# Fused mixer layers on one core: residual sum on TensorE and ScalarE, a shorter routing choice, first group's step sizes ahead of the others

## Chip, core, metric

One core of a Trainium2 chip runs the whole program in one launch. The metric is the device time in microseconds, the median of the runs of one kernel on one chip. TensorE is called PE below, VectorE DVE, ScalarE ACT, GpSimd POOL; SP is the engine that issues most DMAs.

## What is computed

Two layers over 8 sequences of 512 tokens and 256 channels. The change touches only the first half of the first layer, which ends with the routing of the first mixture of experts. Cut to that half:

```python
c   = layernorm((gelu(x @ Wsoma) * sigmoid(temporal(x) @ Wtemp)) @ Wout)   # conditioner
xc, z = split(c @ W_in)                      # 512 + 512 channels
xc  = silu(conv4(xc)); dt, B, C = split(xc @ W_x, [64, 80])
delta = softplus(dt @ W_dt + b_dt)           # per token and channel
for n in 16 states:                          # h, y: 512 channels x 512 tokens
    h_n[t] = exp(delta[t] * A_n) * h_n[t-1] + delta[t] * xc[t] * B_n[t]
    y[t]  += C_n[t] * h_n[t]
x = x + ((y + D * xc) * silu(z)) @ W_out     # residual sum
y0 = x @ Wsub[subject] + bsub
logits = y0 @ Wg + bg; probs = softmax(logits / 5); top 2 of 8; gates normalised
```

`temporal(x)` is a blend of eight causal moving averages of `x * sigmoid(gate)`. Ties at the second largest probability go to the lower expert number.

## The kernel before

The program is a row of blocks, each with one instruction stream for each engine. Streams meet only through semaphores, and every stream is issued in the order in which it is written. The block that matters here is the one that `mixers` makes, with a prologue for batch 0, the eight batches, and after it the short block of `route_last`.

**The scan.** A batch has four groups of 128 channels, and a group four steps. A step `N` (16 in a batch, 128 in all) handles one group and four of the states: DVE makes the input `delta*x*B` (`into`, a product of 128 x 2048), runs the recurrence as one scan over 2048 elements (`scan`), and multiplies the result of the step before by C (`out`). The order in a step is scan N, out N-1, into N+1, and then the small work of `tasks(b, n)`. ACT makes the decays `dA` of step N+2 (`decays`, four exponentials of 511 elements), in `dA`'s two buffers, so decays of N+2 wait for the end of scan N. PE sums the products of the states (`add_state`).

**Around the scan.** While batch b is scanned, its neighbours are worked on in slots `n` = 0 to 15: `k` = b-1 is finished (out product with `Wo`, residual sum `add_out`, subject product, routing), `kc` = b+1 is prepared (conditioner, convolution, delta), and `ke` = b+2 has its gate made. Each engine has a function `tasks(b, n)` that writes out what it does in slot n. `behind` gives k (none for b = 0), `next_up` gives kc (none for b = 7) and ke (none from b = 6).

**The conditioner's averages.** PE turns the gated input (`turn_gated`, line 813), ACT scales and copies it (`scale_turned`, line 920), PE averages (line 822) and takes the block ends (line 829), for eight averages and two halves each, through slots 15, 0, and 2 to 6. These alternate strictly: PE, ACT, PE, ACT. Then come `copy_ends`, `tempo_ready` (line 930), the product with `Wtemp` and the sigmoid `temporal_gate` (line 935). DVE multiplies with it in `soma_gated` (line 988). The products of batch k stand in the same two streams: out product, subject product (`xm,ws`) in two halves, and the logits (`w_Wg,W0u`, 16 small matmuls), on which DVE's `route_maxima` (line 1052) waits.

**Delta to the scan.** `delta_parts` makes |v| and relu(v) on ACT, then exp and ln; `delta_ready` (lines 1002, 1004) sums and multiplies on DVE. The scan needs each channel on four partitions' rows, so delta and u go to HBM (`store_first_group` for group 0, `store_groups` for the other three) and come back spread (`spread_delta`, line 1105, and `spread_u`, line 1114, four DMAs each).

Of the kernel before, what the change touches and what calls it, by code (L numbers as in the profile page):

```python
# [95 lines left out]
def build(nc, a, out):  # L96
    with ExitStack() as ctx:
# [90 lines left out]
        def load_first(st):  # L188
            def sb(name, shape, dt=F32):
# [25 lines left out]
            S4 = sb("S4", [P, LINE])  # L215
            modT = sb("modT", [P, TT, NTR])
# [14 lines left out]
                    mix, Dg, Dc, Rm, S4, modT, f)  # L231
# [190 lines left out]
        def choose_rest(dve, ch, gate_exp, probs, tmp, srt, small, E, K, k=0):  # L422
# [18 lines left out]
            for t in range(TT):  # L441
                ch.step(dve.tensor_tensor_scan(tmp[:, 2, t, :], tmp[:, 1, t, :], tmp[:, 1, t, :], 0.0,
                                               ALU.add, ALU.max))
# [117 lines left out]
        def place_pairs(dve, ch, M, v, bank, limit=False, k=0):  # L561
# [18 lines left out]
            ch.link(dve.tensor_tensor(tmp[:, 1], tmp[:, 1], tmp[:, 0], ALU.mult))  # L580
# [204 lines left out]
        def gate_product(pe, c, k, j):  # L785
            if j == 0:
                pe.wait_ge(c_hg, k + 1)
                pe.wait_ge(c_ctx, DC * (k + 1))
            elif k:
                pe.wait_ge(m_pre, JI * k)  # L790
# [89 lines left out]
        def z_product(pe, k):  # L880
            pe.wait_ge(m_pre, JI * (k + 1))
# [80 lines left out]
        def delta_parts(act, c, k):  # L962
            for j in range(JI):
                act.wait_ge(m_dl, JI * k + j + 1)
                act.activation(c.ab[:, j, :], ps[:, 4 + j, :], ACT.Abs, bias=bdt[:, j:j + 1]).then_inc(m_abs, 1)
                act.activation(c.pre[:, j, :], ps[:, 4 + j, :], ACT.Relu, bias=bdt[:, j:j + 1]).then_inc(m_pre, 1)
# [3 lines left out]
            act.activation(c.ab[:, :, :], c.ab[:, :, :], ACT.Ln, bias=1.0).then_inc(m_ln, 1)  # L970
# [22 lines left out]

        def delta_ready(dve, m, c, k):
            dve.wait_ge(m_pre, JI * (k + 1))
            dve.wait_ge(m_ln, k + 1)
            if k == 0:
                dve.tensor_tensor(c.dl[:, 0, :], c.pre[:, 0, :], c.ab[:, 0, :], ALU.add).then_inc(m_dlr, 1)
                dve.wait_ge(m_dlr, 1)
                dve.tensor_tensor(c.u[:, 0, :], c.dl[:, 0, :], m.xs[:, 0, :], ALU.mult).then_inc(m_u, 1)  # L1000
            j = 1 if k == 0 else 0
            dve.tensor_tensor(c.dl[:, j:, :], c.pre[:, j:, :], c.ab[:, j:, :], ALU.add).then_inc(m_dlr, 1)
            dve.wait_ge(m_dlr, k + 2)
            dve.tensor_tensor(c.u[:, j:, :], c.dl[:, j:, :], m.xs[:, j:, :], ALU.mult).then_inc(m_u, 1)
# [52 lines left out]
        def route_choice(dve, v, ch, k):  # L1057
            choose_rest(dve, ch, r_ex, v.pb[:, :, :], v.tmp, v.srt, v.small, E0, K0, k)
            finish_choice(dve, ch, v.tmp, v.small, E0, K0)
            ch.link(dve.tensor_copy(v.chosen[:, :, :], v.tmp[:, 0]))  # L1060
# [1659 lines left out]
```

## Time and profile before

| | |
|---|---|
| median of 3 runs | 3658.3 us (3652.96 to 3664.64) |
| the profiled execution, its own time | 3662.31 us |
| its span, first to last instruction | 3660.6 us |
| busy in the span | PE 3198.4, DVE 2149.7, ACT 1577.8, POOL 637.8 us |
| mixer block's scans | 144.2 to 1431.4 us |
| TensorE's clock, mean over the span | 0.933 of full |

The spans of the engines overlap, so busy times don't add up. The mixer block takes the first 1446 us, and there DVE is busy in nine tenths or more of nearly every fortieth of the span. What follows (experts, attention, the second layer) isn't touched by the change.

### The profile page before, as it was taken

Reading aid. Unit: us, or ns where it says so; the run is one execution under the profiler, and the core shown is the slowest. Engines: PE = TensorE matmul, PEld = TensorE weight load, DVE = VectorE, ACT = ScalarE, POOL = GpSimd, SP = SyncE. Lnnn points to the kernel's source line nnn. Section 1 sums busy time; section 2 is a strip of 40 time slices with the busy share of each in tenths; the row PEclk is TensorE's granted clock in tenths of the full one; section 3 lists DMA queues with packets and bytes.
Section 4 is the critical chain, followed back from the end, with each engine's and each line's share of the span. In section 5 each row is a group of like instructions: output and inputs, shape, how many; then the busy total and the mean of one; then the engine's idle time right before and its main releaser. Section 6 shows DMA issues by size and latency. Waiting matters only on the chain. (4 is left out here: it accounts for less than half of the span.)

```text
span 3660.6 us, 40917 instructions
## 1 busy us (share of the span) xinstructions
PE 3198.4 (87%) x12812; PEld 1754.9 (48%) x12813; DVE 2149.7 (59%) x2703; ACT 1577.8 (43%) x3071; POOL 637.8 (17%) x767
## 2 busy tenths in 40 slices
PE   8788888888888743899799999999999999978996
PEld 5445353534445211566444444444444444436875
DVE  2499999999999998222233444443434343432334
ACT  4565666666665531333232424242424242423443
POOL 0000202012020202333100202020202020215772
PEclk9898998989898865899899999999999999988998
DMA  2446555555646555322300101010101010055547
GB/s 63 116 120 165 144 146 150 141 153 139 161 122 161 147 140 190 99 67 65 137 0 22 36 22 36 21 37 21 37 21 36 22 37 3 31 208 164 157 156 271
DMA packets 193227, 362.86 MB, mean 99 GB/s; under 512 B 28274, under 2 KB 85106, under 8 KB 191922
## 3 DMA queue, kind: packets, MB, share of 16 engines
q1 hardware_dynamic: 164514, 296.19, 28.2%
q0 software_dynamic: 20352, 57.17, 4.2%
q10 hardware_dynamic: 8208, 7.54, 0.6%
q8 instruction: 85, 1.39, 0.2%
q14 instruction: 68, 0.56, 0.1%
HBM read 250.53 MB, written 110.28 MB: 99 GB/s over the span
## 5 line engine op out<-in xcount | busy, mean ns | idle before, releaser
L1665 DVE TENSOR_TENSOR_SCAN hs<-dA,hs 128x2048 f32<-128x2048 f32 x128 | 566.2, 4423 | 7.1
L452 POOL COPY rows<-slot 128x64 f32<-128x64 f32 x48 | 16.6, 376 | 2592.3 <-DVE new_pl L589 2553.4
L2255 PE MATMUL ps<-pT,V 128*128 128x512 f32 x1024 | 450.7, 593 | 0.9 <-DVE pT L2423 0.9
L1506 ACT ACTIVATE dA<-dl,w_An 128x511 f32<-128x511 f32 x512 | 326.6, 711 | 144.3 <-DVE hs L1665 132.9
L1353 PE MATMUL ps<-hs,w_S 128*32 128x512 f32 x1024 | 176.0, 723 | 169.3 <-DVE hs L1671 169.3
L1657 DVE TENSOR_TENSOR hs<-u,bb 128x2048 f32<-128x2048 f32 x128 | 292.5, 2285 | 19.5 <-DMA u<-ud 9.9
L2255 PEld LDWEIGHTS ps<-pT,V 128*128 128x128 f32 x1024 | 189.6, 190 | 221.1 <-issue 214.8
L1671 DVE TENSOR_TENSOR hs<-hs,cb 128x2048 f32<-128x2048 f32 x128 | 290.4, 2269 | 0.0
L1825 POOL DMA_INDIRECT slots<-og,idt x232 | 241.8, 1042 | 260.2 <-DVE og L1913 197.2
L448 POOL DMA_INDIRECT sorted<-rows,new_pl x192 | 268.2, 1397 | 63.6 <-issue 44.8
L2330 ACT ACTIVATE pp<-ps,nm 128x512 f32<-128x512 f32 x256 | 172.3, 685 | 215.1 <-DVE nm L2406 215.1
L409 PE MATMUL ps<-w_Wv,y 128*128 128x512 f32 x512 | 230.8, 597 | 0.0
L2405 DVE TENSOR_REDUCE mx<-ps 128x4 f32<-128x2048 f32 x64 | 146.4, 2288 | 132.4 <-PE ps L2231 132.4
L813 PE MATMUL ps<-w_mix,W0u 128*128 128x128 f32 x1024 | 165.0, 311 | 52.6 <-ACT W0u L920 39.6
L813 PEld LDWEIGHTS ps<-w_mix,W0u 128*128 128x128 f32 x1024 | 144.4, 216 | 103.1 <-ACT W0u L920 70.0
L920 ACT ACTIVATE W0u<-ps,w_modT 128x256 f32<-128x256 f32 x256 | 106.7, 468 | 176.0 <-PE ps L813 160.6
L409 PE MATMUL ps<-W1u,xT 128*128 x640 | 167.3, 384 | 0.0
L2358 ACT ACTIVATE pT<-ps 128x512 f32<-128x512 f32 x128 | 77.3, 604 | 197.4 <-PE ps L2243 197.4
L2243 PEld LDWEIGHTS ps<-ident,pp 128*128 128x128 f32 x1024 | 115.1, 141 | 90.5 <-issue 61.6
L2423 DVE COPY pT<-ps 128x512 f32<-128x512 f32 x128 | 88.4, 691 | 114.3 <-PE ps L2243 113.7
L822 PE MATMUL ps<-W0u 128*128 128x128 f32 x1024 | 144.5, 291 | 8.8 <-ACT sz L1514 8.8
L1353 PEld LDWEIGHTS ps<-hs,w_S 128*32 128x32 f32 x1024 | 27.8, 117 | 254.3 <-DVE hs L1671 209.6
(355 smaller groups left out, 5389.0 us busy)
## 6 DMA issues: line engine op xcount, KB each, us to landing
bb<-bcd SPq DMA_DIRECT2D x128, 256.0 KB
cb<-bcd SPq DMA_DIRECT2D x128, 256.0 KB
dl<-dld SPq DMA_DIRECT2D x128, 256.0 KB, 6.6
u<-ud SPq DMA_DIRECT2D x128, 256.0 KB, 8.3
xg<-sorted SPq DMA_DIRECT2D x232, 136.0 KB, 2.1
slots<-zeros SPq DMA_DIRECT2D x136, 128.0 KB, 3.8
qrg<-slots SPq DMA_DIRECT2D x32, 512.0 KB, 16.4
rg<-slots SPq DMA_DIRECT2D x32, 256.0 KB, 4.8
```

What stands on the lines that cost most here:

```text
L409: last = pe.matmul(dst, lhsT, rhs, start=(i == 0), stop=(i == len(pairs) - 1))
L448: pool.indirect_dma_start(M.sorted, bass.IndirectOffsetOnAxis(new_pl[:, t, i:i + 1], 0), v.rows[:, i % v.R, t, :], None).then_inc(M.listed ...
L813: ins = pe.matmul(ps[:, turn_bank(k, h), q % 2 * D + j * P:q % 2 * D + (j + 1) * P], c.gated[:, j, q * P:(q + 1) * P], mix[:, j, d, :], st ...
L1353: ins = pe.matmul(ps[LINE * q:LINE * (q + 1), N // GROUP % 3, :], S4[:, :], m.hs[:, N % 3, q, :], start=False, stop=(N % GROUP == GROUP - 1))
L1506: act.activation(m.dA[:, N % 2, q, 1:T], m.dl[:, G % 2, q, 1:T], ACT.Exp, scale=An[:, e, N % GROUP:N % GROUP + 1]).then_inc(s_da, 1)
L1657: dve.tensor_tensor(m.hs[:, N % 3], m.u[:, G % 2], m.bb[:, N % 2, :].unsqueeze(1).to_broadcast([P, GROUP, T]), ALU.mult).then_inc(s_bm, 1)
L1665: dve.tensor_tensor_scan(state, m.dA[:, N % 2].rearrange("p j t -> p (j t)"), state, 0.0, ALU.mult, ALU.add).then_inc(s_h, 1)
L1671: dve.tensor_tensor(m.hs[:, N % 3], m.hs[:, N % 3], m.cb[:, N % 2, :].unsqueeze(1).to_broadcast([P, GROUP, T]), ALU.mult).then_inc(s_pd, 1)
L1825: pool.indirect_dma_start(M.slots, bass.IndirectOffsetOnAxis(idt[:, t:t + 1], 0), og[:, t % 4, :], None).then_inc(M.stored[t % 4], 16)
L2255: ins = pe.matmul(ps[:, 6 + j, :], V[:, m, h * D + j * P:h * D + (j + 1) * P], pT[:, i % 2, h % 2, m, :], start=(h == 0 and m == 0), stop= ...
L2330: act.activation(pp[:, u % 2, s, :], ps[:, s, :], ACT.Exp, bias=nm[:, u % 2, s:s + 1], accum_out=sm[:, u % 2, s:s + 1]).then_inc(p_ex, 1)
L2405: chp.link(dve.tensor_reduce(mx[:, u % 2, :], ps[:, 0:TT, :], X, ALU.max))
```

## The change

1. The residual sum leaves DVE. PE begins each half of the out product with an identity matmul of `xm` (the residual), and ACT copies the finished sum to `xm` in slot 2, after its decays.
2. In the last batch the out product is begun in slot 14, and only the matmuls of the fourth group are left for the end.
3. The routing choice counts ties by one scan over 32 elements with a mask `parted` that cuts it at the tokens' ends, where there were four scans of eight; the five instructions between those scans and the product `wgt` become three.
4. Delta and u are made for group 0 first and then for groups 1 to 3 in every batch (before: only in batch 0), and SP spreads group 0 before it stores the others. In batch 0 relu(v) is made by DVE and ln of group 0 comes first; the spread of batch 0's group 1 moves into slots 0 and 1.
5. The sigmoid `temporal_gate` moves from after to before ACT's decays, `soma_gated` on DVE from after scan 8 of a batch to before it.
6. In slot 15 ACT makes the decays of the next step ahead of `scale_turned(ke, 0, 0)`, and those of the one after it ahead of `scale_turned(ke, 0, 1)`.

```diff
 def choose_rest(..., k=0, parted=None):
+            if parted is not None:
+                ch.step(dve.tensor_tensor_scan(tmp[:, 2]..., parted..., tmp[:, 1]..., 0.0, ALU.mult, ALU.add))
+            for t in range(TT if parted is None else 0):
 def delta_parts(act, c, k):
-                act.activation(c.pre[:, j, :], ps[:, 4 + j, :], ACT.Relu, ...).then_inc(m_pre, 1)
+                if k:
+                    act.activation(c.pre[:, j, :], ps[:, 4 + j, :], ACT.Relu, ...).then_inc(m_pre, 1)
...
+            for j in (0, 1) if k == 0 else (0,):
+                part = slice(0, JI) if k else slice(0, 1) if j == 0 else slice(1, JI)
+                act.activation(c.ab[:, part, :], c.ab[:, part, :], ACT.Ln, bias=1.0).then_inc(m_ln, 1)
 def delta_ready(dve, m, c, k):
+            for i, js in enumerate((slice(0, 1), slice(1, JI))):
+                dve.wait_ge(m_ln, k + 2 if k or i else 1)
+                dve.tensor_tensor(c.dl[:, js, :], c.pre[:, js, :], c.ab[:, js, :], ALU.add).then_inc(m_dlr, 1)
+                dve.wait_ge(m_dlr, 2 * k + i + 1)
+                dve.tensor_tensor(c.u[:, js, :], c.dl[:, js, :], m.xs[:, js, :], ALU.mult).then_inc(m_u, 1)
 def route_choice(dve, v, ch, k):
-            finish_choice(dve, ch, v.tmp, v.small, E0, K0)
-            ch.link(dve.tensor_copy(v.chosen[:, :, :], v.tmp[:, 0]))
-            dve.tensor_tensor(v.wgt[:, :, :], v.tmp[:, 0], v.pb[:, :, :], ALU.mult).then_inc(r_sel, 1)
+            ch.link(dve.tensor_tensor(v.tmp[:, 2], v.tmp[:, 2], v.small[:, 2, :]..., ALU.add))
+            ch.link(dve.scalar_tensor_tensor(out=v.tmp[:, 1], in0=v.tmp[:, 2], scalar=float(K0), in1=v.tmp[:, 1], ...))
+            ch.link(dve.tensor_tensor(v.chosen[:, :, :], v.tmp[:, 0], v.tmp[:, 1], ALU.add))
+            dve.tensor_tensor(v.wgt[:, :, :], v.chosen[:, :, :], v.pb[:, :, :], ALU.mult).then_inc(r_sel, 1)
 SP, n == 14:
                                 store_first_group(sp, c, kc)
-                                store_groups(sp, c, kc)
                                 spread_delta(sp, m, JI * kc, range(GROUP))
                                 spread_u(sp, m, JI * kc, range(GROUP))
+                                store_groups(sp, c, kc)
 PE:
                     def out_product(k):
-                        pe.wait_ge(s_y, JI * (k + 1))
+                        pe.wait_ge(s_x, 16 * (k + 1))
+                        if k == B - 1:
+                            pe.wait_ge(s_y, JI * (k + 1) - 1)
+                        else:
+                            pe.wait_ge(s_y, JI * (k + 1))
                         for j in range(DC):
+                            o = ps[:, out_bank(k, j), :]
+                            pe.matmul(o, ident[:, :], xm[:, j, :], start=True, stop=False)
+                            for i in range(JI - 1):
+                                pe.matmul(o, Wo[:, i, j * P:(j + 1) * P], v.go[:, i, :], start=False, stop=False)
+                            if k < B - 1:
+                                out_last(k, j)
 ACT, n == 2:
                             decays_ahead()
+                            if k is not None:
+                                add_out(k)
                             if kc is not None:
                                 scale_turned(act, c, kc, 2, 1)
 ACT, n == 7 and 8:
                                 tempo_ready(act, c, kc)
+                                temporal_gate(act, c, kc)
                             decays_ahead()
                         elif n == 8:
-                            if kc is not None:
-                                temporal_gate(act, c, kc)
                             decays_ahead()
 DVE, loop:
-                            scan(N)
                             if n == 8 and b + 1 < B:
                                 soma_gated(dve, c, b + 1)
+                            scan(N)
```

ACT's stream in slots 2 and 3 of a middle batch, before. `dA` are the decays, `W0u<-ps,w_modT` the scaled halves of the averages, `W0u<-ps,ws` the bias of the subject product.

```order
L908 ACTIVATE W0u<-ps,w_vec 128x512 x2
L920 ACTIVATE W0u<-ps,w_modT 128x256 x2
L1506 ACT_TABLE_LOAD
L1506 ACTIVATE dA<-dl,w_An 128x511 x4
L920 ACTIVATE W0u<-ps,w_modT 128x256 x2
L1018 ACTIVATE W0u<-ps,ws 128x512
```

And of the change, the same place:

```order
L914 ACTIVATE W0u<-ps,w_vec 128x512 x2
L926 ACTIVATE W0u<-ps,w_modT 128x256 x2
L1543 ACT_TABLE_LOAD
L1543 ACTIVATE dA<-dl,w_An 128x511 x4
L1549 ACTIVATE xm<-ps 128x512 x2
L926 ACTIVATE W0u<-ps,w_modT 128x256 x2
L1028 ACTIVATE W0u<-ps,ws 128x512
```

The two copies that make `xm` stand behind the decays and ahead of the scaled half, and the subject product on PE reads `xm`.

DVE's stream around scan 8 of a batch, before. `hs<-u,bb` is `into`, `hs<-dA,hs` the scan, `hs<-hs,cb` `out`, `W0u<-W0u` `soma_gated`.

```order
L1657 TENSOR_TENSOR hs<-u,bb 128x2048
L1665 SCALAR_TENSOR_TENSOR hs<-dA,hs 128x2048
L988 TENSOR_TENSOR W0u<-W0u 128x512 x2
L1671 TENSOR_TENSOR hs<-hs,cb 128x2048
L1657 TENSOR_TENSOR hs<-u,bb 128x2048
```

And of the change:

```order
L1701 TENSOR_TENSOR hs<-u,bb 128x2048
L997 TENSOR_TENSOR W0u<-W0u 128x512 x2
L1709 SCALAR_TENSOR_TENSOR hs<-dA,hs 128x2048
L1715 TENSOR_TENSOR hs<-hs,cb 128x2048
L1701 TENSOR_TENSOR hs<-u,bb 128x2048
```

The gated product now stands ahead of the scan, so the scan is queued behind its wait for the sigmoid.

SP's stream in slot 14, before. `dld` and `ud` are the copies of delta and u in HBM.

```order
L1089 DMA dld<-W0u 128x512
L1091 DMA ud<-W0u 128x512
L1096 DMA dld<-W0u 128x3x512
L1097 DMA ud<-W0u 128x3x512
L1105 DMA dl<-dld 32x4x512 x4
L1114 DMA u<-ud 32x4x512 x4
```

And of the change:

```order
L1101 DMA dld<-W0u 128x512
L1103 DMA ud<-W0u 128x512
L1117 DMA dl<-dld 32x4x512 x4
L1126 DMA u<-ud 32x4x512 x4
L1108 DMA dld<-W0u 128x3x512
L1109 DMA ud<-W0u 128x3x512
```

The eight spreading DMAs now stand ahead of the two large stores.

## Rows read from the trace of the kernel before

**Rows 1.** Groups of DVE's instructions, 144 to 1440 us: count, busy, mean, idle before.

```profile
L1665 DVE TENSOR_TENSOR_SCAN hs<-dA,hs 128x2048 f32<-128x2048 f32 x128 | 566.2, 4423 | 7.1
```

**Rows 2.** DVE's waits, 144 to 1440 us: in total, times, longest.

```profile
DVE hs L1657 <- DMA u<-ud: 9.9, 1, 9.9
DVE hs L1657 <- issue: 7.5, 7, 1.6
DVE y L992 <- ACT W0u L945: 6.6, 7, 2.7
DVE hs L1657 <- DMA bb<-bcd: 2.1, 1, 2.1
```

**Rows 3.** Timeline of DVE in batch 3: start, duration, instruction, idle before and releaser.

```profile
653.13 2.28 DVE L1657 TENSOR_TENSOR hs<-u,bb 128x2048 f32<-128x2048 f32 x1
...
656.52 4.42 DVE L1665 TENSOR_TENSOR_SCAN hs<-dA,hs 128x2048 f32<-128x2048 f32 x1
...
674.15 0.19 DVE L1052 TENSOR_TENSOR lg<-ps,w_bg 128x32 f32<-128x32 f32 x1
...
685.19 0.41 DVE L442 TENSOR_TENSOR_SCAN tmp<-tmp 128x8 f32<-128x8 f32 x4
...
686.73 0.19 DVE L1061 TENSOR_TENSOR wgt<-tmp,pb 128x32 f32<-128x32 f32 x1
...
703.24 2.28 DVE L1657 TENSOR_TENSOR hs<-u,bb 128x2048 f32<-128x2048 f32 x1
705.63 4.42 DVE L1665 TENSOR_TENSOR_SCAN hs<-dA,hs 128x2048 f32<-128x2048 f32 x1
709.97 1.27 DVE L988 TENSOR_TENSOR W0u<-W0u 128x512 f32<-128x512 f32 x2
...
782.35 4.42 DVE L1665 TENSOR_TENSOR_SCAN hs<-dA,hs 128x2048 f32<-128x2048 f32 x1
```

**Rows 4.** Timeline of ACT in the same batch and at its end.

```profile
632.83 2.56 ACT L1506 ACTIVATE dA<-dl,w_An 128x511 f32<-128x511 f32 x4 [1.32 <-DVE hs L1665]
...
660.19 0.81 ACT L920 ACTIVATE W0u<-ps,w_modT 128x256 f32<-128x256 f32 x2
...
699.13 1.24 ACT L930 ACTIVATE W0u<-ps 128x512 f32<-128x512 f32 x2 [2.36 <-PE ps L836]
...
787.85 0.82 ACT L920 ACTIVATE W0u<-ps,w_modT 128x256 f32<-128x256 f32 x2
```

**Rows 5.** Timeline of PE in batch 2 (the first row) and batch 3.

```profile
476.08 7.03 PE L409 MATMUL ps<-go,w_Wo 128*128 128x512 f32 x16
...
635.03 1.84 PE L1353 MATMUL ps<-hs,w_S 128*32 128x512 f32 x8 [4.40 <-DVE hs L1671]
...
641.02 7.53 PE L409 MATMUL ps<-go,w_Wo 128*128 128x512 f32 x16
...
659.87 1.12 PE L1366 MATMUL ps<-xs,w_Dg 128*128 128x512 f32 x2
...
670.05 1.95 PE L409 MATMUL ps<-w_Wg,W0u 128*128 128x8 f32 x16
...
700.43 3.69 PE L409 MATMUL ps<-W0u,w_Wtemp 128*128 128x512 f32 x8
```

**Rows 6.** Busy by stretch: PE, PEld, DVE, ACT, POOL, then TensorE's granted clock, DMA.

```profile
637.40:641.00 3.60, 3.56 (x16) 3.56 (x17) 3.60 (x2) 3.00 (x4) 0.00 (x0) 0.50 0.88 174
```

**Rows 7.** Timeline of SP's DMA issues at the end of batch 3.

```profile
769.73 0.32 SPq L1089 DMA_DIRECT2D dld<-W0u  x1
...
778.70 1.80 SPq L1114 DMA_DIRECT2D u<-ud  x4
```

**Rows 8.** Timeline of ACT in the prologue.

```profile
123.80 1.91 ACT L970 ACTIVATE W0u<-W0u 128x2048 f32<-128x2048 f32 x1
```

**Rows 9.** Timeline of DVE at the end of the mixer block.

```profile
1442.26 0.69 DVE L1684 TENSOR_TENSOR xm<-xm,ps 128x512 f32<-128x512 f32 x1 [3.86 <-PE ps L409]
1445.62 0.69 DVE L1684 TENSOR_TENSOR xm<-xm,ps 128x512 f32<-128x512 f32 x1 [2.68 <-PE ps L409]
```

More of the change, by code:

```diff
@@ L440, in choose_rest @@
             ch.link(dve.tensor_reduce(small[:, 2, :], tmp[:, 0], X, ALU.add))
-            for t in range(TT):
+            if parted is not None:
+                ch.step(dve.tensor_tensor_scan(tmp[:, 2].rearrange("p t e -> p (t e)"), parted[:, :, :].rearrange("p t e -> p (t e)"),
+                                               tmp[:, 1].rearrange("p t e -> p (t e)"), 0.0, ALU.mult, ALU.add))
+            for t in range(TT if parted is None else 0):
                 ch.step(dve.tensor_tensor_scan(tmp[:, 2, t, :], tmp[:, 1, t, :], tmp[:, 1, t, :], 0.0,
@@ L992, in cond_ready, with first_positive @@
             dve.tensor_tensor(y[:, :, :], c.oc, c.rstd.unsqueeze(1).to_broadcast([P, DC, T]), ALU.mult).then_inc(c_y, 1)
+        def first_positive(dve, c):
+            for j in range(JI):
+                dve.wait_ge(m_abs, j + 1)
+                dve.tensor_scalar(c.pre[:, j, :], ps[:, 4 + j, :], bdt[:, j:j + 1], 0.0, ALU.add, ALU.max).then_inc(m_pre, 1)
         def delta_ready(dve, m, c, k):
             dve.wait_ge(m_pre, JI * (k + 1))
[L996 to L1004, printed above, removed]
+            for i, js in enumerate((slice(0, 1), slice(1, JI))):
[3 more added lines that the diff above has]
+                dve.tensor_tensor(c.u[:, js, :], c.dl[:, js, :], m.xs[:, js, :], ALU.mult).then_inc(m_u, 1)
         def subject_half(pe, b, k, j):
@@ L1248, in next_up, with out_bank @@
                 return b + by if b + by < B else None
+            def out_bank(k, j):
+                return 5 if k == B - 1 and j else (k + 2 + j) % 3
             with nc.Block() as block:
@@ L1286, in _ @@
                     store_groups(sp, c, 0)
-                    spread_delta(sp, m, 1, range(GROUP))
-                    spread_u(sp, m, 1, range(GROUP))
                     for b in range(B):
@@ L1368, in out_product, with out_last @@
                     def out_product(k):
-                        pe.wait_ge(s_y, JI * (k + 1))
-                        for j in range(DC):
-                            product(pe, ps[:, (k + 2 + j) % 3, :], [(Wo[:, i, j * P:(j + 1) * P], v.go[:, i, :])
-                                                                    for i in range(JI)], s_o)
+                        pe.wait_ge(s_x, 16 * (k + 1))
[3 more added lines that the diff above has]
+                            pe.wait_ge(s_y, JI * (k + 1))
+                        for j in range(DC):
+                            o = ps[:, out_bank(k, j), :]
[4 more added lines that the diff above has]
+                                out_last(k, j)
+                    def out_last(k, j):
+                        i = JI - 1
+                        pe.matmul(ps[:, out_bank(k, j), :], Wo[:, i, j * P:(j + 1) * P], v.go[:, i, :],
+                                  start=False, stop=True).then_inc(s_o, 1)
                     def tasks(b, n):
@@ L1493, in _ @@
                     add_state(last - 1)
-                    out_product(B - 1)
+                    pe.wait_ge(s_y, JI * B)
+                    for j in range(DC):
+                        out_last(B - 1, j)
                 @block.scalar
@@ L1507, in decays, with add_out @@
                                            scale=An[:, e, N % GROUP:N % GROUP + 1]).then_inc(s_da, 1)
+                    def add_out(k):
+                        for j in range(DC):
+                            act.wait_ge(s_o, DC * k + j + 1)
+                            act.activation(xm[:, j, :], ps[:, out_bank(k, j), :], ACT.Copy).then_inc(s_xm, 1)
                     def gate_of_z(b):
@@ L1689, in tasks @@
                             gate(k, JI - 1)
-                        elif n == 2 and k is not None:
-                            add_out(k)
                         elif n == 4 and k is not None:
```

55 lines of the change are left out of this document (33 added, 22 removed).

## The prediction, made before the change was run

> **What bounds the kernel now.** I read the grouped DVE rows of the mixer block first, then DVE's waits, then one middle batch (batch 3) on DVE, ACT and PE side by side. The scans alone are 128 x 4.42 us [rows 1]; with `into` (2.28) and `out` a step is 8.9 us, and DVE is almost never idle: its waits in this block sum to some 28 us of 1290 [rows 2]. So DVE sets the time here. Work taken off it is gained, work left elsewhere is free, until something that DVE waits for comes later than DVE wants it. That second half is the question, because PE and ACT alternate through slots 0 to 7 without resting, and the change puts matmuls and copies into that alternation while DVE gets to its meeting points earlier. All sums are against the profiled execution's own 3662.3 us (span 3660.6, so 1.7 around it); that run is 4.0 above the median of 3658.3, and I carry the difference over.
>
> **What DVE is spared.**
> - Residual sum, seven times inside the loop (the eighth is in the tail). From `into` to the next scan: 656.52 - 653.13 = 3.39 with it, 705.63 - 703.24 = 2.39 without [rows 3]. 1.0 x 7 = 7.0.
> - Routing choice. From the first tie scan to `wgt` 1.54 us for nine instructions [rows 3]. Four remain. By the mean they cost 0.69; counting the scans at 0.10 each and the others at 0.22, and one scan of 32 elements at 0.2, 0.87. Saved 0.65 to 0.85; I take 0.65 x 7 = 4.5.
> - The unnamed wait of `into` for u at the start of each batch, 7.5 in seven [rows 2]. SP stores group 0 at 769.73 and issues the last u spread only at 780.5 [rows 7], with the big stores ahead of it in the queue. Now delta of group 0 is ready after a sum over 512 elements (0.69 [rows 9]) and not over 2048 (2.28 [rows 3]), 1.6 us sooner, and nothing but its own store precedes the spread. `into` came at most 1.6 us too early, so the whole 7.5 goes. If the spread is no faster: 0.
> - The wait of y, 6.6 [rows 2]. `soma_gated` stood after scan 8 (709.97); ahead of it, at about 705.5, it starts the product, variance and exponential 4.4 us sooner. Even when the gate is late (below) this is more than the 0.9 us missing per batch, so all 6.6 goes.
> - `soma_gated` between `into` and scan also fills the 0.1 us that DVE idles there (703.24 + 2.28 to 705.63) and overlaps at both ends: 0.2 x 7 = 1.3.
> - Batch 0: SP no longer stands before bb of step 2 waiting for the group stores: 2.1 [rows 2].
> - Prologue. u's arrival ends a wait of 9.9 [rows 2]. ln of one group instead of four: 1.91 x 3/4 less the fixed part, 1.2 [rows 8]; relu of four banks on DVE instead of between the Abs on ACT, so that ACT goes at PE's pace: between 0 and four times 0.6, I take 1.5. Together 2.7.
> - Tail. The last gate ends at 1442.26 - 3.86 = 1438.40, the sum at 1446.31 [rows 9]. Left are two matmuls (0.86 each in two passes, by 7.03/16 = 0.44 a pass [rows 5]) and two copies of 0.6: the sum ends near 1441.0. 5.3 saved.
>
> Sum: 7.0 + 4.5 + 7.5 + 6.6 + 1.3 + 2.1 + 2.7 + 5.3 = 37.0.
>
> **What it adds to DVE.** Delta and u in four instructions instead of two, 0.17 each for two more, on the mean of the nine above: 0.3 x 7 = 2.1 (bounds 0 and 2.6). The tie mask is made by POOL in the prologue, which waits for nobody there.
>
> **What it adds to the alternation of PE and ACT.** For six batches, 1 to 6, both k and kc exist. Batch 3, its times kept on the old axis:
> 1. Slots 15 and 0. The pair that ran at 787.85 now follows decays that wait for the end of the scan begun at 782.35, 786.8, and take 2.55: it starts at 789.3, 1.45 later [rows 3, 4]. DVE's batch starts 1.1 earlier (u wait gone). Against this ACT had 1.3 us of idle time before its decays of step 2 [rows 4]. Net +1.2 against DVE; PE's next matmuls at the lower clock may add up to 1. I take +1.6 (bounds +0.5 and +2.4).
> 4. So the decays of slot 2 end 1.6 - 2.2 + 1.75 = 1.15 later, at 661.3 instead of 660.19 [rows 4]. The two copies take 1.24 like those of line 930 [rows 4], to 662.6. PE's `skip_term` and the subject product wait for them; they began at 659.87 [rows 5]. Now they begin 2.75 later. Copies to ACT cost nothing in themselves; they cost because they are behind the decays, where DVE's sum was done long before.
>
> From there to the sigmoid neither PE nor ACT waits for DVE, so the 2.75 is passed on whole:
> - Logits: ended 672.0 [rows 5], now 674.75. `route_maxima` stood at 674.15 [rows 3] and comes 1.0 sooner. DVE waits 1.6, with scan 5 queued behind it.
> - Gate: product with `Wtemp` ended at 704.1 [rows 5], now 706.9, sigmoids 0.8 more, 707.7. `soma_gated` wants it at the end of `into`, 705.45 - 1.0 - 0.65 = 703.8. Together both waits are 3.9 us, with scan 8 behind the second.
>
> Six batches: 6 x 3.9 = 23.4. Batch 0 has no out product, but its gate is also wanted 4.4 + 2.1 earlier: 1.5 more. Batch 7 has no averages, so ACT copies as soon as PE is done: 0. Bounds per batch: 2.2 with step 1 at its low end and nothing else, 6.1 with no gain in clock.
>
> **Sum.** -37.0 + 2.1 + 23.4 + 1.5 = -10.0, so 3652 against 3662.3, and 3648 on the median's scale. I forecast 3649. Its own range, by the bounds of the alternation (-10, +13) cut to what I hold likely, is 3638 to 3658.
>
> **Two rules weighed.** The copies: two on ACT cost 1.24, DVE's two sums from PSUM 0.69 each [rows 4, 9]. The Trainium skill (ScalarE: Activation LUTs, Rules for kernel authors) says to leave plain adds and multiplies to VectorE, up to three times faster. By that rule the copies would take 3.8 us and lengthen each alternation by 2.6 more, 15 us in all, and the sum would be about +5: no change. The row says 1.24, and these are fp32 from PSUM, so I go by the row.
>
> The clock: [rows 5, 6] show 1.2 GHz behind a pause of 4.4 us. The Trainium skill (TensorE: Matmul & The Clock Gate, HAM oscillation) says that idle gaps throttle the array again and that keeping them short keeps it at full rate; the trace agrees for this gap. Step 2 by that rule is -2.2, without it 0, and the sum would be +3.
>
> **Rivals.**
> - *The clock doesn't recover* (step 2 is 0): waits 6.1 a batch, +13 on the sum: 3665, 3661 on the median's scale, no change. For it: later matmuls in slot 0 begin at the low clock themselves. Against: a shorter pause. 0.12.
> - *The alternation has slack that I don't see*, or the four bounds fall together: DVE waits at most 1 us a batch. -10.0 - 6 x 3 = -28 to -35: 3623 to 3631. Against: in rows 5 and 4 PE and ACT hand over at once. 0.12.
> - *Slower.* PE stays at 1.2 GHz through the whole longer out product: 20 passes at 0.88 instead of 0.44, +8.8 a batch, up to +53, so to 3701. It decides against the change from (10 + 11)/6 = 3.5 us a batch on. For it: `xm` and the fourth gate are waited for there. Against: the out product took 7.0 to 7.5 in batches 2 and 3, and no wait is added before it. 0.06.
> - *The order of stores does nothing for u*: +7.5, 3656 on the median's scale. Inside the likeliest case.
>
> **How the numbers follow.** The likeliest, with new waits of 2 to 5.5 us a batch, has 0.70. A measurement of this kernel tells 0.3%, 11 us, from no change: 3647 and 3669 are the borders. The forecast lies just above the lower one, so I split it 0.38 faster, 0.32 the same. With the rivals: faster 0.38 + 0.12 = 0.50, same 0.32 + 0.12 = 0.44, slower 0.06. The range takes in the first rival and half of the second: 3630 to 3663.
>
> **What would show it.** In the changed kernel's profile: no DVE wait for u in the loop and none at y; DVE's waits at `route_maxima` about 1.6 us and at `soma_gated` about 2.3 us, six times each, both released by the alternation; `xm` copies of 0.6 each right behind decays in slot 2; the granted clock at 1.00 in the averages of slot 1; two short matmul pairs between the last gate and the end of the mixer block. I am wrong if DVE doesn't wait at `soma_gated` (then it is the second rival), if the decays themselves become late for a scan, or if the gate's wait is over 6 us.

## The result, and the profile after

The changed kernel is **slower** by 0.8%: 3688.4 us (median of 6 runs, 3684.8 to 3690.7) against 3658.3 (6 runs, 3653.0 to 3664.6). The ratio is 1.0084, 95% interval 1.0073 to 1.0095. The profiled execution has a span of 3687.9 us. The forecast was 3649, in a range of 3630 to 3663.

The loss lies in batches 1 to 6 of the mixer block: the last scan ends at 1463.4 us of the span, where it ended at 1431.4. First the start of batch 3 and of batch 4 on DVE, then the same engine's waits from 130 to 1480 us (in total, times, longest), to be held against [rows 2].

```profile
636.19 4.42 DVE L1709 TENSOR_TENSOR_SCAN hs<-dA,hs 128x2048 f32<-128x2048 f32 x1
...
806.41 4.42 DVE L1709 TENSOR_TENSOR_SCAN hs<-dA,hs 128x2048 f32<-128x2048 f32 x1
```

```profile
DVE hs L1701 <- PE ps L1373: 40.6, 23, 2.8
DVE hs L1701 <- DMA u<-ud: 11.3, 1, 11.3
DVE W0u L997 <- ACT W0u L941: 10.1, 7, 1.7
DVE go L1722 <- PE ps L1373: 8.0, 7, 2.1
DVE y L1001 <- ACT W0u L951: 2.1, 1, 2.1
...
DVE hs L1701 <- DMA bb<-bcd: 0.4, 1, 0.4
```

Batch 3 takes 806.41 - 636.19 = 170.2 us, and batches 1 to 6 take 168.7 to 171.1; in the trace of before they took 163.1 to 164.5. The waits for u inside the loop are gone (7.5 before), those of y fell from 6.6 to 2.1, those for `bb` from 2.1 to 0.4. In their place `into` waits 40.6 us for `add_state` on PE, twenty-three times: PE's stream comes late, with the sums of states queued behind the averages. Who makes PE late stands in ACT's waits, same stretch, and in ACT's timeline at the end of batch 2:

```profile
ACT W0u L926 <- PE ps L818: 106.0, 64, 3.9
...
ACT dA L1543 <- DMA dl<-dld: 40.3, 7, 7.0
ACT W0u L926 <- DMA ud<-W0u: 40.0, 7, 7.3
```

```profile
626.69 2.56 ACT L1543 ACTIVATE dA<-dl,w_An 128x511 f32<-128x511 f32 x4 [4.77 <-DMA dl<-dld]
635.17 0.84 ACT L926 ACTIVATE W0u<-ps,w_modT 128x256 f32<-128x256 f32 x2 [5.92 <-DMA ud<-W0u]
635.90 2.55 ACT L1543 ACTIVATE dA<-dl,w_An 128x511 f32<-128x511 f32 x4
638.35 0.82 ACT L926 ACTIVATE W0u<-ps,w_modT 128x256 f32<-128x256 f32 x2
```

The second row is the main part of the case. `scale_turned(ke, 0, 0)` writes into the tiles that delta and u of the next batch still occupy, so it waits for the stores `ud<-W0u` that read them. Before, the last of those stores went out at 609.07 and took 6.8 us to land, and the scale, at 620.88, had waited for PE. Now SP issues them behind the eight spreading DMAs. SP's issues at the same place:

```profile
612.15 0.53 SPq L1089 DMA_DIRECT2D bb<-bcd  x1
612.81 0.40 SPq L1101 DMA_DIRECT2D dld<-W0u  x1
613.48 0.33 SPq L1103 DMA_DIRECT2D ud<-W0u  x1
619.98 1.75 SPq L1117 DMA_DIRECT2D dl<-dld  x4
621.83 1.80 SPq L1126 DMA_DIRECT2D u<-ud  x4
623.72 0.39 SPq L1108 DMA_DIRECT2D dld<-W0u  x1
624.16 0.54 SPq L1109 DMA_DIRECT2D ud<-W0u  x1
```

The last store goes out at 624.16 and lands 10.9 us later, where it took 6.8 before, and ACT gets on at 635.17, right behind the landing. The Trainium skill (DMA: Bandwidth & Descriptors, Queues, rings and completion order) says that a DMA's semaphore is written only after every earlier write of the same DMA engine, by which the stores' end stands behind the eight spreads ahead of them; the longer landing agrees with it.

TensorE's clock. The averages of slot 1 with the pause ahead of them, before and then in the changed kernel, and the stretch 651.40 to 654.80 by engine (the clock is the number behind POOL's):

```profile
637.44 3.78 PE L822 MATMUL ps<-W0u 128*128 128x128 f32 x16 [0.56 <-ACT sz L1514]
```

```profile
651.38 3.46 PE L827 MATMUL ps<-W0u 128*128 128x128 f32 x16 [4.37 <-ACT sz L1556]
```

```profile
651.40:654.80 3.40, 3.40 (x17) 3.40 (x18) 3.40 (x3) 3.37 (x5) 0.00 (x0) 0.56 0.27 80
```

The pause is as long as the 4.40 us of before [rows 5], but it stands in another place. That one was ahead of the sum of states, for `out`, with only 0.56 us more ahead of the averages. Now the sum of states follows without a pause, and the averages wait 4.37 us for the first `sz`, which ACT makes behind the late scales and decays. The clock is 0.56.

The routing choice and the tail, on DVE (first and last row), ACT (the copies) and PE:

```profile
700.04 0.22 DVE L443 TENSOR_TENSOR_SCAN tmp<-w_parted,tmp 128x32 f32<-128x32 f32 x1
...
700.97 0.19 DVE L1073 TENSOR_TENSOR wgt<-chosen,pb 128x32 f32<-128x32 bf16 x1
...
1469.89 0.69 DVE L1722 TENSOR_TENSOR go<-ps,sz 128x512 f32<-128x512 f32 x1 [2.06 <-PE ps L1373]
```

```profile
675.31 1.05 ACT L1549 ACTIVATE xm<-ps 128x512 f32<-128x512 f32 x2
...
1474.45 0.60 ACT L1549 ACTIVATE xm<-ps 128x512 f32<-128x512 f32 x1 [1.11 <-PE ps L1404]
```

```profile
1470.63 3.78 PE L1404 MATMUL ps<-go,w_Wo 128*128 128x512 f32 x4 [0.81 <-DVE go L1722]
```

From tie scan to `wgt` 0.93 us instead of 1.54: the choice saves 0.6 a batch, as forecast. From the end of the last gate (1470.58) to the end of `xm` (1475.05) 4.5 us instead of 7.9: 3.4 saved of 5.3 forecast, since the two products left for PE take four passes of 0.94 us (3.78), where I had counted 0.44 a pass. They run at a granted clock of 0.50; before, all sixteen passes of the out product stood here and ran at 1.00.

### The profile page after: what moved, and what is told of

Read it like the earlier page. It is cut to its first block and busy times, and to the rows that moved or that the text cites. A ratio compares the mean times of both kernels' runs of the same rounds, so it can differ in the third digit from the quotient of the medians.

```text
span 3687.9 us, 40978 instructions
## 1 busy us (share of the span) xinstructions
PE 3215.4 (87%) x12844; PEld 1761.6 (48%) x12845; DVE 2142.7 (58%) x2670; ACT 1584.7 (43%) x3084; POOL 653.3 (18%) x769
## 5 line engine op out<-in xcount | busy, mean ns | idle before, releaser
L1701 DVE TENSOR_TENSOR hs<-u,bb 128x2048 f32<-128x2048 f32 x128 | 292.7, 2286 | 52.3 <-PE ps L1373 40.6
L452 POOL DMA_INDIRECT sorted<-rows,new_pl x192 | 281.5, 1466 | 63.6 <-issue 44.8
L827 PEld LDWEIGHTS ps<-W0u 128*128 128x128 f32 x1024 | 134.1, 206 | 38.2 <-ACT sz L1556 37.3
```

What stands on the lines that cost most here:

```text
L452: pool.indirect_dma_start(M.sorted, bass.IndirectOffsetOnAxis(new_pl[:, t, i:i + 1], 0), v.rows[:, i % v.R, t, :], None).then_inc(M.listed ...
L827: pe.matmul(ps[:, 6 + j, q * P:(q + 1) * P], c.turned[d % 2][:, q, j * P:(j + 1) * P], c.decay[:, d, :], start=(d == 0 and q == 0), stop=F ...
L1701: dve.tensor_tensor(m.hs[:, N % 3], m.u[:, G % 2], m.bb[:, N % 2, :].unsqueeze(1).to_broadcast([P, GROUP, T]), ALU.mult).then_inc(s_bm, 1)
```

## The experiments

The theory after the traces: the late stores hold up ACT's scale in slot 15 and with it the whole alternation. The rival: the copies, the identity matmuls and the low clock did it, since the stores only move a wait that was there. Ratios below are to the kernel before.

**1. Stores first again.** The changed kernel with SyncE's old order.

```diff
                                 store_first_group(sp, c, kc)
+                                store_groups(sp, c, kc)
                                 spread_delta(sp, m, JI * kc, range(GROUP))
                                 spread_u(sp, m, JI * kc, range(GROUP))
-                                store_groups(sp, c, kc)
```

> The change with one thing undone: in slot 14 SP again stores groups 1 to 3 before it spreads group 0. Theory S (stores): scale_turned of slot 15 overwrites the tiles that hold delta, so it waits for all stores; behind eight spreading DMAs they land some 6 us too late, and that is the loss. Then 3688 falls by 6 batches x 5.5 = 33, and up to 7.5 of u waits come back: 3655 to 3663, with no wait of ACT for the stores and DVE waits of some 4 us a batch, as I had worked out. Rival C (copies and matmuls): the two ACT copies and the identity matmuls in the alternation of PE and ACT cost far more than the 3 us I gave them. Then 3682 or more, as before the undoing.

3663.3 us, 1.0017 (1.0007 to 1.0026): **25.1 us back by one moved line**. ACT, DVE and PE at the same place, then DVE's waits:

```profile
619.50 2.56 ACT L1543 ACTIVATE dA<-dl,w_An 128x511 f32<-128x511 f32 x4 [6.69 <-DMA dl<-dld]
621.97 0.82 ACT L926 ACTIVATE W0u<-ps,w_modT 128x256 f32<-128x256 f32 x2
...
625.13 0.82 ACT L926 ACTIVATE W0u<-ps,w_modT 128x256 f32<-128x256 f32 x2
```

```profile
627.08 4.42 DVE L1709 TENSOR_TENSOR_SCAN hs<-dA,hs 128x2048 f32<-128x2048 f32 x1
```

```profile
633.74 1.06 PE L1373 MATMUL ps<-hs,w_S 128*32 128x512 f32 x8 [2.25 <-DVE hs L1715]
636.86 3.78 PE L827 MATMUL ps<-W0u 128*128 128x128 f32 x16 [2.06 <-ACT sz L1556]
```

```profile
DVE hs L1701 <- PE ps L1373: 22.4, 13, 2.6
...
DVE W0u L997 <- ACT W0u L941: 10.1, 7, 1.7
...
DVE go L1722 <- PE ps L1373: 2.1, 1, 2.1
```

The second pair of scales runs 2.0 us ahead of the batch's first scan (625.13 against 627.08). In the changed kernel it ran 2.2 behind it (638.35 against 636.19), so the late stores push the alternation back by 4.1 us against DVE: six times that is 24.7, the 25.1 measured. DVE's waits say the same: those for PE, at `into` and at `go`, fall from 48.6 to 24.5 us. The u waits, of which up to 7.5 us could have come back, don't: one of 1.0 us is left. So with group 0's delta made first, u comes in time in either order of the stores, and the move of the stores bought nothing. What is left of the loss is another matter. ACT waits 6.69 us for delta's spread ahead of the decays (before, 9.12 for PE ahead of the scale), and the averages still take 3.78 us, behind pauses of 2.25 and 2.06 with the sum of states between them at full clock.

**2. Late stores alone.** The kernel before with only the order of the stores changed.

```diff
                                 store_first_group(sp, c, kc)
-                                store_groups(sp, c, kc)
                                 spread_delta(sp, m, JI * kc, range(GROUP))
                                 spread_u(sp, m, JI * kc, range(GROUP))
+                                store_groups(sp, c, kc)
```

> The kernel before with this one thing of the change: SP spreads group 0 before it stores groups 1 to 3. Theory S: PE's and ACT's alternation starts 6 us late; before there were 2 us of slack at the logits and 3.7 at the gate, so DVE waits about 4 us in each of six batches, less 1.1 of u wait: +15 to +25, 3673 to 3683. Rival C: only the u waits go, 3651 to 3656.

3670.5 us, 1.0031 (1.0018 to 1.0043): 12.0 slower. ACT and DVE's waits:

```profile
631.72 0.84 ACT L920 ACTIVATE W0u<-ps,w_modT 128x256 f32<-128x256 f32 x2 [12.71 <-DMA ud<-W0u]
```

```profile
DVE hs L1665 <- ACT dA L1506: 14.3, 6, 3.2
...
DVE hs L1657 <- PE ps L1353: 6.8, 9, 1.1
DVE y L992 <- ACT W0u L945: 3.5, 3, 2.8
```

Here the scale stands ahead of the decays, so the decays are held up too, and the scan waits for them, up to 3.2 us. The waits of `into` for u, 7.5 us, are gone, and those of y are 3.1 us less. The order of the stores is a net loss by itself, in either kernel, though less here than the 15 to 25 us expected.

**3. The residual sum back on DVE**, all else as changed (DVE's `add_out` in slot 2 and in the tail, no identity matmuls, no copies).

```diff
 PE, out_product:
-                            pe.matmul(o, ident[:, :], xm[:, j, :], start=True, stop=False)
...
 ACT, add_out:
-                            act.activation(xm[:, j, :], ps[:, out_bank(k, j), :], ACT.Copy).then_inc(s_xm, 1)
...
 DVE, add_out:
+                            dve.tensor_tensor(xm[:, j, :], xm[:, j, :], ps[:, (k + 2 + j) % 3, :], ALU.add).then_inc(s_xm, 1)
```

> The change with the residual sum back on DVE in slot 2 and at the end (no identity matmuls, no ACT copies, nothing of the out product in slot 14). Theory S: the alternation is 3 us shorter in six batches (1.75 of matmuls, 1.24 of copies), DVE has 7 x 1.0 more to do, the tail is 4 longer: 3688 - 18 + 7 + 4, partly hidden in the waits, 3678 to 3685. Rival C: the loss is gone, 3655 to 3662.

3673.8 us, 1.0042 (1.0025 to 1.0059): 14.6 less than the changed kernel, below the range that I expected and far above the rival's. So here, where the alternation is late, PE's and ACT's share of the sum costs more than DVE's did.

**4. Delta's stores early, u's late.** Delta of groups 1 to 3 is stored ahead of the spreads and u behind them, each on a semaphore of its own, and the scale waits for delta's stores alone. The tiles that hold u are written only in slot 3, and ACT waits for u's store there.

```diff
                                 store_first_group(sp, c, kc)
+                                store_groups(sp, c, kc)
                                 spread_delta(sp, m, JI * kc, range(GROUP))
                                 spread_u(sp, m, JI * kc, range(GROUP))
-                                store_groups(sp, c, kc)
+                                store_u_groups(sp, c, kc)
...
 ACT, scale_turned:
-                    act.wait_ge(m_st, 32 * k)
+                    act.wait_ge(m_st, 16 * k)
...
 ACT, n == 3:
+                            if b >= 0:
+                                act.wait_ge(m_su, 16 * (b + 1))
```

> The change with the store of groups 1 to 3 parted: delta's goes ahead of the spreads, u's stays behind them, each with a semaphore of its own; scale_turned, which overwrites delta alone, waits for delta's store only, and the subject's bias of slot 3, which overwrites u, for u's. Theory S: the alternation starts on time and the u waits stay away: 3648 to 3658, at or a little below the kernel with the stores first. Rival C: 3682 or more.

3660.3 us, 1.0004 (0.9994 to 1.0014): 28.2 less than the changed kernel, level with the kernel before, and 2 us above the range expected. One of the two large stores still stands behind the spreads here, so the loss hangs on what the scale waits for, and not on bytes moved late.

**5 to 8. The rest of the loss, one edit after the other.** Each of the next three kernels is the one ahead of it with one more edit, from that of experiment 1 on.

```diff
 ACT, n == 2 (5):
+                            if k is not None:
+                                add_out(k)
                             if kc is not None:
                                 soma_ready(act, c, kc)
...
                             decays_ahead()
-                            if k is not None:
-                                add_out(k)
 ACT, n == 15 (6):
-                            elif kc is not None:
-                                decays_ahead(1)
                             if ke is not None:
                                 scale_turned(act, c, ke, 0, 0)
-                            decays_ahead()
+                            if kc is not None:
+                                decays_ahead(1)
                             if ke is not None:
                                 scale_turned(act, c, ke, 0, 1)
+                            decays_ahead()
 DVE, loop (7):
+                            scan(N)
                             if n == 8 and b + 1 < B:
                                 soma_gated(dve, c, b + 1)
-                            scan(N)
```

> The changed kernel with SyncE's order restored (the stores of groups 1 to 3 ahead of the eight spreading transfers in slot 14) and, besides, ScalarE's two copies of the out product moved from behind the decays of slot 2 to the start of slot 2, where ScalarE idles. Theory A: the copies lengthen ScalarE's chain of slot 2 by about 1.1 to 1.25 us in each batch; moved, they fall into idle time, and the time is 3656 (six batches, about 1.2 us each, below the 3663.3 of the kernel with the stores restored). Rival B: the copies cost nothing where they stood, since ScalarE waits for the soma weights behind them anyway: 3663. Rival C: the out product is late and ScalarE now waits for it ahead of the soma gate: 3668 or more, with a wait of the copies for TensorE in the table of waits.

3653.8 us, 0.9991 (0.9982 to 1.0): 9.5 less than experiment 1, or 7.8 when each is held against the kernel before in its own runs (table below). ACT's copies, each behind PE, where the kernel of experiment 1 idled 8.5 us for PE's soma product:

```profile
646.80 0.60 ACT L1549 ACTIVATE xm<-ps 128x512 f32<-128x512 f32 x1 [2.33 <-PE ps L1404]
651.09 0.60 ACT L1549 ACTIVATE xm<-ps 128x512 f32<-128x512 f32 x1 [3.69 <-PE ps L1404]
```

> As the run with ScalarE's copies first, and with slot 15 of ScalarE as in the kernel before: the first scaling of the turned group stands ahead of the decays of the next batch's first step. Theory A: the decays wait 6 to 7 us for the landing of delta's spread; with the scaling ahead of them, the scaling and its consumer on TensorE start before that landing, and each batch ends 2 to 4 us sooner: 12 to 24 us less than the run with the copies first, 3635 to 3645. Rival B: the scaling then waits for the stores instead, since it overwrites what they read, and the decays start later: no gain or a loss, 3656 to 3662.

3650.7 us, 0.9982 (0.9973 to 0.9991): 3.2 less, at the edge of what the runs tell apart, and far from the 12 to 24 expected. The scale went ahead of the decays' wait and was then released by PE. The swap of slot 15 was nearly harmless once the stores stood first.

> As the run with the scaling ahead of the decays, and with the soma multiplication of VectorE behind the scan of slot 8, as in the kernel before, instead of ahead of it. Theory A: VectorE waits 1.7 us in each batch for ScalarE's gate ahead of scan 8 (10.1 us in all), because ScalarE's chain is longer than the scans that cover it; behind the scan that wait is gone, and the multiplication lands about as early: 5 to 10 us less than the run before it, with the wait for ScalarE's gate absent from the table. Rival B: the chain of the averages that follows the soma product ends last, so the product made later delays everything by the 3.9 us of a scan: the time is 5 to 20 us more.

3641.8 us, 0.9959 (0.9946 to 0.9973): 8.8 less. The wait for the gate (10.1 before) is gone from the table, and 3.7 us more are waited at y:

```profile
DVE y L1001 <- ACT W0u L951: 5.8, 4, 3.1
DVE hs L1701 <- PE ps L1373: 5.0, 6, 1.1
```

**8.** All three, on the stores of experiment 4.

> The changed kernel with delta's store of groups 1 to 3 ahead of the spreading transfers and u's store behind them, the copies first in slot 2, the scaling ahead of the decays in slot 15, and the soma multiplication behind scan 8. Theory A (each of the four is a separate term of the loss): 3625 to 3640, below both kernels, and a few us below the run with the stores restored and the soma multiplication behind the scan, because delta's spread lands sooner. Rival B: the terms stand on one another, and what is left of the loss lies in TensorE's longer work at a low clock: 3650 to 3660.

3639.1 us, 0.9953 (0.9940 to 0.9967): faster than both kernels, 17.6 us below the kernel before in the same runs (3656.7).

**9. TensorE's pause filled.** Experiment 8 with the skip term of group 0 made seven times more in slot 0, overwritten each time.

```diff
                             if b >= 0:
-                                skip_term(b, 0)
+                                skip_term(b, 0, b > 0)
...
                             if b > 0:
+                                for _ in range(5):
+                                    skip_term(b, 0, True)
                                 add_state(NS * b - 1)
+                                skip_term(b, 0, True)
+                                skip_term(b, 0)
```

> The kernel of the run with all four edits, with TensorE's idle time ahead of the last sum of states in slot 0 filled: the skip term of group 0 (one product of 128x512, about 0.53 us at the full clock) is made seven times more in each of batches 1 to 7, its result overwritten each time. Nothing of the output changes. In the kernel before and in the changed one the granted clock falls to 0.50 some 6 to 9 us behind the first scan of each batch, behind an idle time of 2.7 to 4.4 us, and the averages (3.7 to 3.8 us for 16 instead of half of that) and half of the out product lie in it. Theory A: with the idle time filled the clock stays 1.00 there, the averages take 2.0 us, the chain to the out product is 1.5 to 3 us shorter, and the time is 3626 to 3635. Rival B: the clock stays up, but the chain of slots 1 to 8 has slack by now: 3639 within 3 us. Rival C: the clock falls all the same, and the seven products only delay the sum of states: 3642 to 3650.

3636.4 us, 0.9944 (0.9930 to 0.9958). The averages in experiment 8, then PE around them here, and the stretch 630.20 to 632.10:

```profile
629.58 3.70 PE L828 MATMUL ps<-W0u 128*128 128x128 f32 x16 [0.74 <-ACT sz L1562]
```

```profile
623.00 4.46 PE L1392 MATMUL ps<-xs,w_Dg 128*128 128x512 f32 x10
627.39 1.06 PE L1379 MATMUL ps<-hs,w_S 128*32 128x512 f32 x8
628.38 1.98 PE L1392 MATMUL ps<-xs,w_Dg 128*128 128x512 f32 x4
630.21 1.95 PE L828 MATMUL ps<-W0u 128*128 128x128 f32 x16
```

```profile
630.20:632.10 1.90, 1.90 (x18) 1.89 (x17) 1.90 (x1) 1.88 (x3) 0.00 (x0) 1.00 0.69 146
```

The averages take 1.95 us at the full clock, where they took 3.70. The lower clock is real and costs about 1.8 us on PE at this place, but the kernel gets only 2.7 us in all (3.9 against the kernel before in the same runs): about the bound of rival B, within the overlap of the two intervals. That PE has time to spare at that place by then fits, but it is argued. (A product of two passes takes 0.9 us here, 4.46 for ten passes, and not the 0.53 expected.)

**10. The residual sum back on DVE in the kernel of experiment 8** (the edit of experiment 3).

> The kernel of the run with all four edits, but the residual sum back on VectorE (two sums of 128x512 behind slot 2, no identity products on TensorE, no copies on ScalarE, the tail as in the kernel before). Theory A: moving the sum off VectorE is a gain once its copies stand where ScalarE idles: VectorE's two sums cost about 1 us a batch on the scans' engine and the tail 5 us, so that this kernel needs 3647 to 3652. Rival B: the sum moved is worth nothing in the batches, since the identity products lengthen TensorE's chain by as much: only the tail's 4 to 5 us come back, 3643 to 3645.

3645.4 us, 0.9971 (0.9961 to 0.9981): 6.2 more than with the sum moved, though the two intervals just overlap. In both traces the last scan ends at 1413.1 us, so the batches don't gain from the move in this pair. The spans differ by 4.2 us (3641.6 and 3637.4), all of it behind the last scan. The profiled execution here was the fastest of nine (3643.4), so where the other 2 us lie isn't shown.

**11. The soma multiplication ahead of scan 8, in the kernel before.**

```diff
-                            scan(N)
                             if n == 8 and b + 1 < B:
                                 soma_gated(dve, c, b + 1)
+                            scan(N)
```

> The kernel before with one edit alone: VectorE's soma multiplication ahead of the scan of slot 8 instead of behind it. Theory A: in the kernel before, ScalarE's gate comes so late that VectorE waits 1 to 2 us for it in each batch ahead of the scan, and the half of a scan that the chain of the averages wins does not pay for it: 3661 to 3668, with a wait for the gate of about 7 to 12 us in all. Rival B: the move is a small gain by itself, as the forecast had it (about 1.3 us): 3655 to 3658, with no wait for the gate.

3657.8 us, 1.0001 (0.9992 to 1.0010): nothing. The time lies in rival B's range, but there is a wait for the gate, which B had at nothing. DVE's waits show the trade, 4.5 us less at y [rows 2] and 5.7 for the gate:

```profile
DVE W0u L988 <- ACT W0u L935: 5.7, 7, 0.8
DVE y L992 <- ACT W0u L945: 2.1, 1, 2.1
```

**12. Late stores in the kernel of experiment 7**: the edit of experiment 2.

> The kernel of the run with the soma multiplication behind the scan (copies first, scaling ahead of the decays, 3641.8), but with SyncE's order of the changed kernel: the stores of groups 1 to 3 behind the eight spreading transfers in slot 14. The late stores cost 25.1 us in the changed kernel and 12.0 us in the kernel before. Theory A (ScalarE's two waits of slot 15 add up): in the changed kernel the decays wait first for delta's landing and the scaling behind them waits on for the stores; with the scaling first there is one wait, the scaling's chain starts at the same time as in the kernel before with late stores, and the cost is about 12 us: 3652 to 3656. Rival B (the cost is that of the landing, whatever stands in slot 15): about 25 us, 3664 to 3670, since the scaling waits till some 635 us of the span either way and the next decays now wait behind it.

3675.4 us, 1.0048 (1.0034 to 1.0061): 33.5 more than experiment 7 (32.5 against the kernel before in the same runs). Both expectations fell. ACT and DVE's waits:

```profile
629.83 0.84 ACT L926 ACTIVATE W0u<-ps,w_modT 128x256 f32<-128x256 f32 x2 [14.70 <-DMA ud<-W0u]
```

```profile
DVE hs L1701 <- PE ps L1373: 20.6, 18, 1.4
DVE hs L1709 <- ACT dA L1543: 17.1, 6, 3.8
```

With the scale first, its long wait makes the decays late too, and `into` waits for PE besides. In the changed kernel no scan waits for its decays, so the swap of slot 15 shielded the scans from that part of the late stores. How much it saved isn't shown, as this kernel differs from the changed one in the copies and the soma product too.

Why the same edit costs 33.5 us here and 12.0 in the kernel before can be read from the waits. Here the decays bring 17.1 us, PE at `into` 15.6 more than in experiment 7 (20.6 against 5.0) and y 1.4 more, and only 1.6 of u waits go: 32.5. In experiment 2 the decays bring 14.3 and PE at `into` 6.8, but 7.5 of u waits and 3.1 at y go: 10.5, and 1.9 more are waited in the tail. What makes PE later for `into` here than there stays open.

## Why the prediction was wrong

**The step that failed** is the first one of the sum on the alternation, "Slots 15 and 0", which I priced at 1.6 us a batch (bounds 0.5 and 2.4). It had the scale start 2.5 us ahead of the next batch's first scan, and it started 2.2 us behind it. The step named the decays ahead of the scale, and neither what the scale overwrites nor what else was moved past it. The stores of groups 1 to 3 appear in the text only as something taken out of u's way. SP's queue was read for what comes sooner, not for what comes later. The wait for those stores is worth 4.1 us a batch and 25.1 us in all (experiment 1), and no rival held it: "the decays themselves become late for a scan", among the signs of being wrong, came nearest.

The rest, point by point:

- *Step 1 without the stores* was right. Forecast was a scale 2.5 us ahead of the next batch's first scan (789.3 against a first scan 1.1 us sooner than 792.86); experiment 1 shows 2.0.
- *Step 2, the clock,* was wrong. The pause for `out` did shrink, from 4.40 to 2.25 us (experiment 1), as forecast. But the averages wait for ACT's `sz` besides, which the prediction didn't count, and that pause grew from 0.56 to 2.06; the averages still took 3.78. That a pause of about 2 us is short enough had no row behind it. The Trainium skill's rule on idle gaps (TensorE: Matmul & The Clock Gate, HAM oscillation) pointed the right way, since filled pauses do give the full clock (experiment 9). Without the 2.2 a batch my sum gave 3661, the first rival, and the changed kernel with the stores in order needs 3663.3. That the clock is what separates it from 3649 is argued: where it was set right, in a kernel with slack, it gave 2.7 us.
- *Where DVE waits.* Forecast were 1.6 us a batch at `route_maxima` and 2.3 at `soma_gated`, 24.9 with batch 0. No trace has the first: just ahead of `route_maxima` DVE already waits up to 2.6 us at `into`, for the sum of states that PE makes behind the subject product. The prediction never took `add_state` for a meeting point. In experiment 1 `into` waits 22.4 us and the gate 10.1, 32.5 together. That is 7.6 of the 14 us between 3649 and 3663.3; the tail adds 1.9 and a wait left at y 2.1.
- *Copies behind the decays*: priced 1.24 a batch, so 7.4; moved into idle time they gave 9.5, or 7.8 against the kernel before in the same runs (experiment 5). Right in kind and in size. The pair took 1.05 us. The Trainium skill (ScalarE: Activation LUTs, Rules for kernel authors) gives its "up to about 3×" for bf16 and operations with one source. The prediction left that condition out, so its 3.8 us for these fp32 copies isn't what the page says, and no trace shows it; its sum went by the row, rightly.
- *The gate's wait*: forecast 2.3 us a batch, measured 1.4 (10.1 in seven). The scan queued behind it made the earlier place a loss of 8.8 us in this kernel and of nothing in the kernel before (experiments 7, 11), where the sum had booked 6.6 and 1.3 as gains against it.
- *The residual sum*: 7.0 was booked as DVE's gain and 1.75 and 1.24 a batch as costs of PE and ACT. In the kernel of experiment 8 the net is nothing in the batches (experiment 10); in the changed kernel, where the alternation is late, it is a loss (experiment 3). The tail gains 3.4 us by the trace, not 5.3, as its products ran at a clock of 0.50.
- *Right*: no wait for u in the loop (though the move of the stores wasn't needed for it, experiment 1), the choice at 0.6 a batch, `bb`, and that DVE's waits move to PE and ACT.

| kernel | us | step | kernel before, same runs | difference to it |
|---|---|---|---|---|
| changed | 3688.4 | | 3658.3 | +30.2 |
| + stores first | 3663.3 | -25.1 | 3658.5 | +4.9 |
| + copies first in slot 2 | 3653.8 | -9.5 | 3656.7 | -2.9 |
| + scale ahead of decays | 3650.7 | -3.2 | 3656.7 | -6.1 |
| + soma behind the scan | 3641.8 | -8.8 | 3656.7 | -14.9 |
| + delta's store early, u's late | 3639.1 | -2.7 | 3656.7 | -17.6 |
| + TensorE's pause filled | 3636.4 | -2.7 | 3657.9 | -21.5 |

The runs were made on several chips, and the kernel before varied by 1.7 us between them, so a step from one chip to another is uncertain by about as much. The step of 3.2 and the last two are each within the overlap of neighbouring intervals. Other parts of the change (choice, first group, prologue, tail, batch 0) weren't undone one by one; together with the sum they are worth 15 to 18 us, by the rows with the soma product and delta's store.

## What to carry to other kernels

When a transfer is moved later in a queue, list who waits for its end, not only who waits for its data: a store also frees the tile that it reads, and the next writer of that tile may stand at the head of a chain. Keep a wait out from ahead of what the bound engine needs: the steps of the table that paid removed no work, they moved it into idle time or took a wait from in front of it. When two edits aim at one wait, try each alone: here either one ended the waits for u, and the second cost 25 us. Taking work off the busiest engine is worth only what the engines that receive it can hide.

## What the runs showed of the hardware

- **The landing of a small store went with the load ahead of it.** In the changed kernel u's store of group 0 went out at 613.48 and its reader, the first spread, was issued at 619.98, 6.5 us later. Before it was 772.00 to 774.81 [rows 7], 2.8 us. What differs is the load of `bb`, which went out 1.3 us ahead of the store in the one (612.15 above) and 4.5 us ahead in the other. In all the traces here, seven batches each, the first spread follows that load by 6.9 to 8.6 us: with the load 1.3 us ahead of the store, the store takes 6.1 to 7.2 us, with 4.5 us ahead 2.3 to 3.7. No run moved the load alone.
- **A pause of 2.06 us, behind one of 2.25, and the clock was at its lower level.** In experiment 1 the granted clock was 1.00 in the sum of states between the two pauses (633.74 to 634.80) and 0.50 in the averages behind them (3.78 us for sixteen products). With seven products put into the pauses it was 1.00 in the averages (1.95 us, experiment 9).
- **Two copies of 128x512 from PSUM on ScalarE took 1.05 us back to back**, 0.60 each when apart; VectorE's sum of the same size took 0.69 [rows 9].
